# A two-layer macaron block on one core: the order of the steps on all five engines written anew

## The reference, cut to what matters

```
x = x + 0.5 * ffn_q(layernorm(x))        # q: rows scaled and rounded to whole numbers, one 128x128 product
x = x + attn0(layernorm(x))              # f: conv over 4 taps, gated linear recurrence (RG-LRU), output product,
                                         # m: then h1 + down(gelu(gate(u)) * up(u)), hidden width 512
x = x + 0.5 * ffn_q(layernorm(x))        # q again
x = x + 0.5 * moe(layernorm(x))          # r, e, x, t, c
x = x + attn1(layernorm(x))              # g: state = state * g_t + k_t v_t^T, out = q_t state, output product
x = x + 0.5 * moe(layernorm(x))          # r, e, x, t, c
```

```python
shared = _expert(x, Wg_s, Wu_s, Wd_s)
probs = jax.nn.sigmoid(jnp.einsum('bsh,eh->bse', x, Wr) + rb)
scores, idx = jax.lax.top_k(probs, TOP_K)
out = shared + sum over e of cw[..., e:e + 1] * _expert(x, Wg[e], Wu[e], Wd[e])
```

## Time and profile before

| | before |
|---|---|
| median of 3 runs | 807.21 us |
| the profiled execution's own time | 805.45 us |
| its span | 802.4 us |
| PE busy | 647.6 us, 81% |
| DVE busy | 512.9 us, 64% |
| ACT busy | 396.1 us, 49% |
| POOL busy | 385.1 us, 48% |
| granted clock of PE, mean | 0.953 of full |

### The profile page before, as it was taken

One profiled execution on the slowest core, in us unless ns is written; L12 is line 12 of the kernel. 1 busy time (PEld: TensorE's weight loads), 2 busy tenths in 40 slices (PEclk: granted clock), 3 DMA queues, 4 the chain that ended last, 5 costly groups with the idle time before them and its releaser, 6 DMA issues.

```text
span 802.4 us, 14619 instructions
## 1 busy us (share of the span) xinstructions
PE 647.6 (81%) x4312; PEld 508.4 (63%) x4312; DVE 512.9 (64%) x1704; ACT 396.1 (49%) x975; POOL 385.1 (48%) x401
## 2 busy tenths in 40 slices
PE   1377999996789888897896679899899998877850
PEld 0234556455457677796884467768777997766840
DVE  5879868667788466364233897977854874742315
ACT  1267687984964634543452606255247324434430
POOL 3327345246655167677562412174634733574540
PEclk9997999998999999999999699999999999999985
DMA  9992000000313246566775300013343343446839
GB/s 333 411 411 94 1 1 1 1 14 21 103 30 91 62 110 180 159 188 199 215 230 143 90 1 1 2 55 107 111 135 104 117 121 103 119 133 181 236 127 290
DMA packets 73566, 100.98 MB, mean 126 GB/s; under 512 B 10417, under 2 KB 45105, under 8 KB 73233
## 3 DMA queue, kind: packets, MB, share of 16 engines
q1 hardware_dynamic: 64848, 82.21, 34.3%
q0 software_dynamic: 8640, 17.84, 6.1%
HBM read 61.79 MB, written 38.23 MB: 125 GB/s over the span
## 4 chain that ended last, share of the span: by engine, by line
PE 51%; DVE 12%; POOL 10%; issue 10%; DMA 7%; ACT 6%; SPq 3%; POOLq 0%; DVEq 0%; ACTq 0%
PE bank L971 10%; POOL rows_by_expert L769 6%; PE bank L952 5%; PE bank L1171 4%; PE bank L290 4%; PE bank L629 3%; PE bank L464 3%; PE bank L615 3%; PE bank L866 2%; PE bank L852 2%; DMA tin<-rows_by_expert 2%; PE bank L644 2%; PE bank L841 2%; PE bank L295 2%; DMA rows_done<-tout,tin 2%
## 5 line engine op out<-in xcount | busy, mean ns | idle before, releaser
L971 PE MATMUL bank<-tint,twt 128*128 128x128 f32 x1136 | 153.6, 279 | 8.1 <-DVE thidt L1010 7.9
L769 POOL DMA_INDIRECT rows_by_expert<-xx,sidx x128 | 125.7, 982 | 71.3 <-DVE xx L752 35.5
L971 PEld LDWEIGHTS bank<-tint,twt 128*128 128x128 f32 x1136 | 140.3, 194 | 10.4 <-DVE thidt L1010 9.7
L1021 POOL DMA_INDIRECT rows_done<-tout,tin x98 | 95.1, 970 | 100.7 <-ACT tout L994 79.0
L1010 DVE TENSOR_TENSOR thidt<-tsil,bank 128x256 f32<-128x256 f32 x142 | 58.9, 419 | 106.5 <-ACT tsil L989 75.6
L952 PE MATMUL bank<-e_dn,thidt 128*128 x568 | 90.8, 283 | 18.8 <-issue 14.2
L952 PEld LDWEIGHTS bank<-e_dn,thidt 128*128 128x128 f32 x568 | 77.3, 193 | 40.1 <-issue 39.9
L989 ACT ACTIVATE tsil<-bank 128x256 f32<-128x256 f32 x142 | 54.5, 384 | 89.7 <-PE bank L971 89.4
L982 ACT ACTIVATE tint<-bank 128x128 f32<-128x128 f32 x142 | 39.3, 277 | 88.7 <-PE bank L958 88.3
L1171 PE MATMUL bank<-bufA,bufB 128*128 128x128 f32 x448 | 62.2, 288 | 8.0 <-DVE at L1196 3.8
L1171 PEld LDWEIGHTS bank<-bufA,bufB 128*128 128x128 f32 x448 | 56.5, 200 | 12.6 <-DVE tseg L1193 6.4
(11 more groups left out here) (253 smaller groups left out, 1387.7 us busy)
## 6 DMA issues: line engine op xcount, KB each, us to landing
twt<-moe_gu SPq DMA_DIRECT2D x142, 256.0 KB
rows_by_expert<-tout SPq DMA_DIRECT2D x25, 715.0 KB, 20.1
tin<-rows_by_expert SPq DMA_DIRECT2D x142, 65.0 KB, 2.5
hid<-rows_done SPq DMA_DIRECT2D x24, 256.0 KB, 4.8
x<-x_in SPq DMA_DIRECT2D x4, 512.0 KB, 6.8
rows_by_expert<-xx,sidx POOLq DMA_INDIRECT x128
out<-x SPq DMA_DIRECT2D x8, 256.0 KB, 4.8
rows_done<-tout,tin POOLq DMA_INDIRECT x98, 2.4
```

The source lines that it names most:

```text
L769: pool.indirect_dma_start(out=rows_by_expert, out_offset=bass.IndirectOffsetOnAxis(ap=sidx[h][:, k:k + 1], axis=0), in_=xx[h][:, r, t, :], ...
L971: m = pe.matmul(bank[UP_BANKS[p][j]][:, c * P:(c + 1) * P], weights[:, c * P:(c + 1) * P], tint[g % TURNS][:, :], start=True, stop=True)
L1021: pool.indirect_dma_start(out=rows_done, out_offset=bass.IndirectOffsetOnAxis(ap=dst, axis=0), in_=tout[:, g % RING, :], in_offset=None).t ...
```

## The change

Every engine keeps its steps, each once, with its waits and its buffers; only the order in which the five lists call them is another. 204 of SP's 311 calls stand at another place, by -4 to +5 places; 546 of 611 on DVE (by up to 33 up and 38 down among those that do work); 128 of 251 on POOL (-5 to +32); 475 of 569 on PE (-21 to +31); 383 of 451 on ACT (-15 to +28). The two lists of an engine meet again at the same calls many times. The places that the prediction speaks of, POOL in layer 0 first:

```diff
     f_xh_gpsimd(pool, 4)
-    f_root2_gpsimd(pool, 4)
     f_b_gpsimd(pool, 5)
     q_root_gpsimd(pool, 1, 1)
+    q_bias_gpsimd(pool, 2, 1)
+    f_xh_gpsimd(pool, 5)
+    f_root2_gpsimd(pool, 5)
+    f_b_gpsimd(pool, 6)
     r_scatter_gpsimd(pool, 0, 0, 0)
-    f_root2_gpsimd(pool, 5)
-    q_bias_gpsimd(pool, 2, 1)
     r_scatter_gpsimd(pool, 0, 0, 1)
-    f_b_gpsimd(pool, 6)
     q_bias_gpsimd(pool, 3, 1)
-    f_xh_gpsimd(pool, 5)
     f_xh_gpsimd(pool, 6)
+    f_root2_gpsimd(pool, 6)
+    r_root_gpsimd(pool, 1, 0)
+    f_b_gpsimd(pool, 7)
     r_scatter_gpsimd(pool, 1, 0, 0)
-    f_root2_gpsimd(pool, 6)
     r_scatter_gpsimd(pool, 1, 0, 1)
-    f_b_gpsimd(pool, 7)
-    r_root_gpsimd(pool, 1, 0)
-    f_xh_gpsimd(pool, 7)
+    q_root_gpsimd(pool, 2, 1)
     f_root2_gpsimd(pool, 7)
-    q_root_gpsimd(pool, 2, 1)
-    r_scatter_gpsimd(pool, 2, 0, 0)
     q_bias_gpsimd(pool, 4, 1)
    ...
+    for j in range(9, 14):
+        t_store_gpsimd(pool, 0, j)
     r_scatter_gpsimd(pool, 5, 0, 0)
-    for j in range(9, 11):
-        t_store_gpsimd(pool, 0, j)
+    r_scatter_gpsimd(pool, 5, 0, 1)
     q_bias_gpsimd(pool, 7, 1)
-    t_store_gpsimd(pool, 0, 11)
-    r_scatter_gpsimd(pool, 5, 0, 1)
-    for j in range(12, 15):
+    for j in range(14, 18):
         t_store_gpsimd(pool, 0, j)
     r_root_gpsimd(pool, 3, 0)
-    for j in range(15, 26):
+    for j in range(18, 26):
         t_store_gpsimd(pool, 0, j)
     r_scatter_gpsimd(pool, 6, 0, 0)
-    for j in range(26, 28):
+    for j in range(26, 30):
         t_store_gpsimd(pool, 0, j)
     r_scatter_gpsimd(pool, 6, 0, 1)
-    for j in range(28, 34):
+    for j in range(30, 37):
         t_store_gpsimd(pool, 0, j)
     r_scatter_gpsimd(pool, 7, 0, 0)
-    for j in range(34, 36):
-        t_store_gpsimd(pool, 0, j)
     r_scatter_gpsimd(pool, 7, 0, 1)
```

ACT, around the roots of units 5 and 6:

```diff
-    f_yb_scalar(act, 6)
-    r_apply_scalar(act, 1, 0)
-    f_sa_scalar(act, 6)
-    f_tx_scalar(act, 7)
-    f_sqrt_scalar(act, 5)
-    r_rows_scalar(act, 1, 0)
     f_exp_scalar(act, 6)
     f_square_scalar(act, 6)
+    f_sqrt_scalar(act, 5)
+    r_apply_scalar(act, 1, 0)
+    f_sqrt_scalar(act, 6)
+    x_scalar(act, 1, 0)
+    m_gelu_scalar(act, 4, 0)
     f_si_scalar(act, 6)
-    m_gelu_scalar(act, 4, 0)
-    e_silu_scalar(act, 0, 0, 0)
     f_xc_scalar(act, 7)
     m_gelu_scalar(act, 4, 1)
-    f_sqh_scalar(act, 5)
     m_gelu_scalar(act, 4, 2)
     r_xt_scalar(act, 1, 0)
+    m_gelu_scalar(act, 4, 3)
+    e_silu_scalar(act, 0, 0, 0)
+    f_sqh_scalar(act, 5)
     f_yb_scalar(act, 7)
-    m_gelu_scalar(act, 4, 3)
     f_u_scalar(act, 5)
+    f_ut_scalar(act, 5)
+    r_tanh_scalar(act, 1, 0)
     q_copy_scalar(act, 2, 1)
-    r_tanh_scalar(act, 1, 0)
-    f_sqrt_scalar(act, 6)
```

DVE, at the start, at the first table, and at the start of layer 1:

```diff
+    q_stats_vector(dve, 2, 0)
+    k_first_vector(dve)
     q_whole_vector(dve, 0, 0)
     q_scale_vector(dve, 1, 0)
     q_whole_vector(dve, 1, 0)
+    q_limits_vector(dve, 2, 0)
+    q_out_vector(dve, 0, 0)
     k_weights_vector(dve)
-    q_out_vector(dve, 0, 0)
+    x_vector(dve, 0, 0)
+    q_stats_vector(dve, 3, 0)
     f_stats_vector(dve, 0)
-    q_limits_vector(dve, 2, 0)
     q_out_vector(dve, 1, 0)
+    k_decay_vector(dve)
     f_stats_vector(dve, 1)
     f_mom_vector(dve, 0)
     q_limits_vector(dve, 3, 0)
-    q_stats_vector(dve, 2, 0)
-    q_stats_vector(dve, 3, 0)
+    q_stats_vector(dve, 4, 0)
    ...
+    f_h1_vector(dve, 7)
     table_vector(dve, 0, 0)
-    m_hid_vector(dve, 5, 1)
-    f_scan_vector(dve, 7)
-    m_hid_vector(dve, 5, 2)
-    f_hy_vector(dve, 7)
-    e_hid_vector(dve, 0, 0, 1)
-    m_hid_vector(dve, 5, 3)
-    f_h1_vector(dve, 7)
    ...
     g_stats_vector(dve, 3)
+    c_add_vector(dve, 5, 0)
+    c_add_vector(dve, 6, 0)
+    g_value_vector(dve, 0)
     g_mom_vector(dve, 1)
-    e_add_vector(dve, 7, 0)
-    c_add_vector(dve, 4, 0)
-    c_add_vector(dve, 5, 0)
-    g_stats_vector(dve, 4)
-    g_stats_vector(dve, 5)
-    g_mom_vector(dve, 2)
-    g_value_vector(dve, 0)
+    g_first_vector(dve, 0)
     g_value_vector(dve, 1)
-    g_first_vector(dve, 0)
     g_first_vector(dve, 1)
-    c_add_vector(dve, 6, 0)
     g_level_vector(dve, 0, 0)
```

SP, loads of tiles against loads of weights in layer 0 (tiles 40 to 48) and layer 1 (24 to 29, 41 to 46), and the last fetch:

```diff
     t_weights_sync(sp_, 0, 39)
-    t_load_sync(sp_, 0, 41)
+    for j in range(41, 45):
+        t_load_sync(sp_, 0, j)
     t_weights_sync(sp_, 0, 40)
-    for j in range(42, 44):
-        t_load_sync(sp_, 0, j)
-    for j in range(41, 43):
+    t_load_sync(sp_, 0, 45)
+    for j in range(41, 46):
         t_weights_sync(sp_, 0, j)
-    t_load_sync(sp_, 0, 44)
-    t_weights_sync(sp_, 0, 43)
-    t_load_sync(sp_, 0, 45)
-    for j in range(44, 46):
-        t_weights_sync(sp_, 0, j)
-    for j in range(46, 48):
+    for j in range(46, 49):
         t_load_sync(sp_, 0, j)
     for j in range(46, 49):
    ...
         t_weights_sync(sp_, 1, j)
+    for j in range(24, 29):
+        t_load_sync(sp_, 1, j)
+    t_weights_sync(sp_, 1, 24)
+    t_load_sync(sp_, 1, 29)
     for j in range(25, 28):
+        t_weights_sync(sp_, 1, j)
+    t_load_sync(sp_, 1, 30)
+    for j in range(28, 30):
+        t_weights_sync(sp_, 1, j)
+    for j in range(31, 33):
         t_load_sync(sp_, 1, j)
-    t_weights_sync(sp_, 1, 25)
    ...
+    t_weights_sync(sp_, 1, 41)
+    t_load_sync(sp_, 1, 44)
+    for j in range(42, 46):
+        t_weights_sync(sp_, 1, j)
+    t_load_sync(sp_, 1, 45)
+    t_weights_sync(sp_, 1, 46)
+    for j in range(46, 51):
         t_load_sync(sp_, 1, j)
-    t_weights_sync(sp_, 1, 41)
-    t_load_sync(sp_, 1, 45)
-    t_weights_sync(sp_, 1, 42)
-    t_load_sync(sp_, 1, 46)
-    t_weights_sync(sp_, 1, 43)
-    t_load_sync(sp_, 1, 47)
-    t_weights_sync(sp_, 1, 44)
-    t_load_sync(sp_, 1, 48)
-    t_weights_sync(sp_, 1, 45)
    ...
     c_fetch_sync(sp_, 6, 1)
+    o_store_sync(sp_, 0)
     c_fetch_sync(sp_, 7, 1)
-    o_store_sync(sp_, 0)
```

More of the change, by code:

```diff
@@ new lines, in _ @@
+            t_load_sync(sp_, 0, 14)
+            t_weights_sync(sp_, 0, 14)
+            t_load_sync(sp_, 0, 15)
+            for j in range(15, 17):
+                t_weights_sync(sp_, 0, j)
+            for j in range(16, 19):
+                t_load_sync(sp_, 0, j)
+            t_weights_sync(sp_, 0, 17)
+            for j in range(19, 22):
+                t_load_sync(sp_, 0, j)
+            t_weights_sync(sp_, 0, 18)
+            t_load_sync(sp_, 0, 22)
+            t_weights_sync(sp_, 0, 19)
@@ L2119, in _ @@
+            g_last_vector(dve, 7)
+            x_vector(dve, 1, 28)
+            taken_vector(dve, 1, 2)
             g_add_vector(dve, 6)
```

1866 lines of the change are left out of this document (941 added, 925 removed).

## The result

The changed kernel takes 765.13 us in the median of 4 runs (764.29 to 766.85), the kernel before, measured beside it, 806.37: a ratio of 0.950 (95% interval 0.947 to 0.954), 41 us less. Forecast were 11 us less, 796, with 783 as the lower end of the range. The direction was right and the size wrong by a factor of nearly four.

What follows compares the result with a forecast made beforehand. PE, busy 81%, was taken as the bound, with gains only from its 154.8 us idle plus clock costs. Layer 0's -7.3 and layer 1's -5.1 gave -12.4, cut to -11 for double counting: 796 us, range 783 to 808.

Steps and rivals of the forecast that it cites:

- ACT's term: Table loads fall from 40 to 34, nearly all between 63 and 240 us; 2.6 us gained, some 1.4 probably counted twice.
- first tiles: Layer 0: table(0,0) and unit 1's scatters come later, so PE reaches x(0,0) with about 3.5 us missing: +3.5.
- waves, end of layer 0: Later scatters +1.2 for x(0,25) to x(0,49), shared-expert steps +2.6 of PE, SP's loads ahead of tile 40's weights +1.
- x(1,25): Layer 1: SP's loads 25 to 28 come ahead of weights 24, and load 28 waits for store 16: +3.3, bounds 0 and 7.
- f_b(6): POOL, 158 to 240 us: put ahead of both scatter steps, it can start about 8 us earlier than 185.89.
- PE's idle time in the middle: Sign that the forecast is right: PE's idle in its 158 to 240 us stretch, 15.2 before, falls under 9 us.
- Carried forward by hand, m_up(6,2) ... comes 10 to 14 earlier. But DVE then becomes dense ... I take 8.5.: 158 to 240 us, largest term: 8.5 us gained, cut from 10 to 14 for DVE; bounds 0 and 15.2, PE's idle time.
- rival C: All comes through: 5.19 us gap gone, PE at full clock, hand timeline's 12 instead of 8.5; about 788 us, chance 0.22.
- Later r_rank(5,0) ... -3.3: Layer 0: r_rank(5,0) no longer stands ahead of x(0,11) on DVE, where PE waited 3.30 at 289.58: -3.3.
- -2.8 ... -2: Layer 1 start: c_add(6,0) and g_stats(0) moved, -2.8; earlier routing of unit 0 and a shared-expert step filling gaps, -2.
- layer 0 ... shorter by 5 to 10 us at the first step of layer 1: Sign that the forecast is right: the changed trace reaches layer 1's first step 5 to 10 us sooner.
- late ... -4 net: Late layer 1: weights 44 ahead of load 47, units 6 and 7 pulled up, shared-expert steps cost PE 2.6: -4, bounds -8 and +3.

Runs made afterwards that it cites:

- a_wo2: Changed kernel with three SP calls moved back (weights of tile 40 in layer 0 and tile 24 in layer 1, last fetch): 767.18 us beside the changed kernel's 768.17.
- n_l0rest: Kernel before, with the new order only among steps between 232 and 447 us of its trace (tiles of layer 0): 794.99 us against 805.46, ratio 0.988.
- u_mid2: Changed kernel with the old order restored among steps between 127 and 221 us (middle of layer 0): 784.43 us, beside the changed kernel's 768.17.
- n_l1: Kernel before, with the new order only from 447 us of its trace to the end (layer 1): 789.76 us against 805.46, ratio 0.981.
- n_mid: Kernel before, with the new order only among steps between 130 and 232 us of its trace: 799.33 us against 805.46, ratio 0.993.
- n_f6: Kernel before with four steps moved up (f_left(6), f_ix(6), f_sqrt(6), f_b(6)): 906.28 us against 904.75, ratio 1.001.
- n_clock: Kernel before, with five unused PE matmuls added for unit 6 in the wait before f_mix(6): 905.33 us against 904.75, ratio 0.999.
- n_fb: Kernel before with one POOL call moved, f_b(6) ahead of r_scatter(0,0,1) instead of behind it: 895.48 us against 897.12, ratio 1.001.

## Why the prediction was wrong

The forecast and the result by stretches, in us; the forecast's terms are grouped by place (the middle has 8.5 and the 1.2 left of ACT's term), the measured ones are differences of the table's row "changed", with the last tile and the end from the chain of waits:

```
stretch, by PE work done                  forecast   measured
up to 119 (start, 63 to 158 us)             -1.2       -3.1
119 to 149 (middle)                         -9.7      -15.7
149 to 164 (first tiles)                    +3.5       +3.5
164 to 238 (to tile 25)                     -3.3      -12.3
238 to 328 (waves, end of layer 0)          +4.8       +6.3
328 to 432 (layer 1 to the tiles)           -4.8      -13.6
432 to 507 (around x(1,25))                 +3.3       +2.9
507 to the last tile                        -4.0       -7.1
the last fetch and adds                     +0.4       -0.4
sum                                        -11.0      -39.5
```

*Held.* The table loads: 34, as counted (the split that was given for them adds up to 36: e_silu was to go from 5 to 6 and went to 4). f_b(6): 178.09, 7.8 us earlier, against "about 8". The wait of 5.19 went. PE's idle time in the middle is 5.5, under the 9 named as a sign. The waves and the end of layer 0: forecast 4.8, measured 11.4 given back from 238 to 283 and 5 of it won again, 6.3 in all.

*Right in the number, not in the reason.* First tiles: PE finds the rows of x(0,0) at 220.09 without a wait, where 2 to 5 us were foreseen. The 3.5 that the table shows there are two other waits, for ACT's f_u of unit 6 (2.32) and for a product of DVE (1.41), and slow matmuls behind the first (2.07 us at 205.44 for a pair that takes 1.02 to 1.13 elsewhere; granted clock 0.50 from 206 to 208). x(1,25): +2.9 against +3.3, but a_wo2, with the weights of tile 24 ahead of the loads again, loses as much there (+3.0), so SP's order isn't the cause; it stays open. Both agreements are luck.

*Failed: "Carried forward by hand, m_up(6,2) ... comes 10 to 14 earlier. But DVE then becomes dense ... I take 8.5."* m_up(6,2) comes 14.5 earlier, with the first tiles already behind it:

```profile
225.56 1.02 PE L629 MATMUL bank<-ut,w_gu 128*128 128x512 f32 x2
```

Up to this place the forecast had 8.5 + 1.2 - 3.5 = 6.2, all of it idle time. Measured are 9.7 of idle time and 4.7 of PE's busy time. Two steps were wrong.

The discount: DVE did become dense, 59.96 us of 67.6 where 62.3 of 68 were feared, and PE's waits stayed away all the same; a busy share says nothing of which wait ends last. And part of DVE's 62.3 us wasn't work but stretching by POOL, 3.8 us in this scan and table(0,0) alone (between the two rows lies one operation, L798, of 1.70 that takes 0.22 in the changed kernel), and it goes when the order does.

The clock: the window's 0.94 was read and carried only in rival C, 5 us, as if it were a matter of chance; in the sum it stood at nothing, though the low clock came with the wait and went with it. The upper bound of the term, PE's idle time there, was no bound for the same reason. That the hand timeline's 14 met 14.5 is in part luck too: nothing in it made a matmul shorter. Rival C (788) had the mechanism, and was priced at one place.

*Failed: "Later r_rank(5,0) ... -3.3" as the whole gain between the first tiles and tile 25.* It was 12.3, and n_l0rest and u_mid2, which have the new order there and the old one in the middle, win as much (12.1 and 12.2). The kernel before waits 3.30, 1.16, 2.27 and 2.64 at PE between 289 and 324, 1.47 at 261.9, and has a clock of 0.83 from 290 to 300; the changed kernel has 1.6 in two waits. I priced the one for which I found a moved step, and zero for the rest.

*Failed: layer 1, "-2.8 ... -2".* From the end of layer 0 to 432 of PE's work the changed kernel wins 13.6, and n_l1 alone as much. The first level of the recurrence: DVE's last add before it, and PE.

```profile
429.33 0.69 DVE L1045 TENSOR_TENSOR x<-x,hid 128x512 f32<-128x512 f32 x1
...
439.38 2.32 PE L1171 MATMUL bank<-bufA,bufB 128*128 128x128 f32 x16
```

The wait of 2.74 is gone. c_add(6,0) was priced at 2.2 us from a row that says 1.64 for its second add; the same add takes 0.69 here. Behind it the old trace has ten more waits of 0.6 to 1.6 us between 484 and 585 (10.2 us together), the changed one six of 0.5 to 1.4 in the same work (5.1); I counted 2. PE's work is shorter here as well: the 448 matmuls of L1171 take 59.7 us instead of 62.2. So the sign "layer 0 ... shorter by 5 to 10 us at the first step of layer 1" failed: that step comes at 439.38 instead of 465.83.

*Half right: "late ... -4 net".* The direction held, and 4.3 us are won up to 581 of PE's work, but 7.1 up to the last tile. The forecast charged PE 2.6 us for the shared-expert steps of unit 7 that go to the end. The last of them, e_down(7,1), now runs behind the last tile, while SP fetches and PE has nothing else to do, so it costs nothing:

```profile
746.29 3.78 PE L866 MATMUL bank<-e_dn,ehid 128*128 128x128 f32 x16 [11.16 <-DVE ehid L860]
```

*The layer and the parts.* The sum of single terms is also wrong as a form: n_mid gives 6 us alone and 16.3 when it is the part missing. n_mid's lead was lost behind its cut, to two waits for ACT and the low clock behind them. How much of that belongs to the old list and how much to the seam wasn't told apart.

So the miss is one habit: gains only where I could name a moved step, losses everywhere I could imagine one, and PE's busy time taken as fixed. Between the first 63 and the last 27 us PE stood idle for 90 us; in the changed kernel, with the same two stretches left out, for 60.

## What to carry to other kernels

When a whole schedule is replaced, stalls share causes, and the gains of single stalls don't add up to the whole: the middle measured alone gave 6.1 us, and 16.3 when it was the part missing. Replaying all five lists with their durations would be the better estimate, but that wasn't tried; the one stretch followed came out at 10 to 14 against 14.5, and a discount on a busy share made it worse. Before calling an engine dense, look for instructions of one line with unlike lengths: the long ones can be another engine's doing and leave with the old order. And a single call moved to kill a stall need not show in the total: n_f6, n_clock and n_fb each changed the stall as meant, or in part, and none moved the total beyond its interval.
